# A third-order feature interaction kernel: first chunk in halves, D groups ahead of c1, q weights of chunks 0 to 3 on VectorE

## The chip, the cores and the metric

One core of one Trainium2 chip. A core has TensorE (matmuls, into PSUM), VectorE, ScalarE, GpSimd, and SyncE, which here only issues DMAs. The metric is the device time of one execution in microseconds; lower is better.

## The reference

Input x is (B=512, M=40, D=16). W0, W1, W2 are (40, 40, 100), (40, 100, 100), (40, 100, 100); b0 to b2 have 100 entries, lin_w 300.

```python
curr = x
for Wk, bk in zip([W0, W1, W2], [b0, b1, b2]):
    z = einsum('bid,bjd->bdij', x, curr)
    curr = einsum('bdij,ijh->bhd', z, Wk) + bk[None, :, None]
    logit.append(curr)
out = sum(concatenate(logit, axis=1), axis=-1) @ lin_w + lin_b     # (512, 1)
```

## The kernel before

Only layer 1's output c1 is computed in full. The sum over d makes layers 2 and 3 a quadratic form: out = sum over d and h of c1 times q, where q is a product of the same pairwise terms z with weights D, and D is built on the chip from W1, W2 and lin_w. A constant feature (the 41st) and an extra output column (the 101st, J=101) carry the biases.

**Chunks.** z is symmetric in i and j, so 41 features give some 880 pairs, held as C=7 chunks of K=126 rows. The columns are N=1024: two d values of 512 examples. There are U=8 such column blocks, so NCH=56 chunks, numbered m = 7u + c. For each chunk VectorE forms z = x_a * x_b (`form`, line 246), ScalarE rounds it to the 32-bit matmul type as z_high (`round_high`, L324), and VectorE makes z_low = z - z_high (`split`, L253). TensorE then does three products (high x high, low x high, high x low) in two halves of 512 columns, six matmuls, once with the c1 weights (`c1_chunk`) and once with the q weights (`q_chunk`), both L434. The q products run LAG=8 chunks behind the c1 products.

**x_b.** In chunks 1 to 6 it is picked out of x_a by a selection matmul (`select_xb`, L476). From chunk 7 on it comes by DMA: `load_xb(1, c)` brings x for chunk 7 + c into xb_z[c], once chunk c has been split (low_done), so chunk 9 uses `load_xb(1, 2)`, chunk 10 `load_xb(1, 3)`.

**D.** `v_piece`, `turn_v` and v_sb reduce W2 and lin_w to v. Five D groups (`d_group`, L518 and L521, two matmuls each) multiply W1 by v into two PSUM buffers in turn; ScalarE copies each out (`copy_d`, L338) before its buffer is used again. SyncE and GpSimd store the groups to DRAM (`store_d`, L159), and once all stores have landed nine gathers by SyncE and three by ScalarE (`gather_d`, L153) bring them back in pairs: piece 0 holds the two sides for chunks 0 and 1, piece 1 for chunks 2 to 6. The q weights are the sum of both sides, then rounded (wq_high), then the remainder (wq_low). VectorE does that for chunks 0 and 1 (`first_weights`, L279 to L284), GpSimd for chunks 2 and 3 and for 4 to 6 (L419 to L424).

**Order.** It is written by hand, each engine works through its own list, and semaphores tie them. VectorE's list in the first loop body is form(m), then for m = 9 `first_weights`, then split(m-1). TensorE's list begins with 20 matmuls on zeros (`warm`, L485), selections, v pieces and c1 chunk 0, then D groups 0 and 1, c1 chunk 1, D groups 2 and 3, selection 6, D group 4, c1 chunks 2 to 7, and then q(0), c1(8), q(1), c1(9) and so on. SyncE's list around the change is the part that matters most:

```python
            store_d(sp, 0, LEFT + 4 * GI, 4 * GI, LOWER - 4 * GI, d_stored)
            sp.wait_ge(low_done, 3)
            load_xb(1, 2)
            sp.wait_ge(equals_cleared, 1)
            sp.wait_ge(d_stored, 16 * DS)
            sp.wait_ge(d_stored_pool, 16)
            for side, t, piece in GATHER:
                if piece == 1 and (side, t) == (0, 0):
                    sp.wait_ge(low_done, 4)
                    load_xb(1, 3)
```

Of the kernel before, what the change touches and what calls it, by code (L numbers as in the profile page):

```python
# [42 lines left out]
PREP_AT = 9  # L43
# [5 lines left out]
WARM = 20  # L49
# [10 lines left out]
def build(nc, xa, xw, w0_pairs, w1x, w2h, small, out):  # L60
# [3 lines left out]
    with ExitStack() as ctx:  # L64
# [54 lines left out]
        xa_loaded = [sem(f"xa_loaded{i}") for i in range(2)]  # L119
        w0_loaded = [sem(f"w0_loaded{i}") for i in range(len(WC_CUTS) - 1)]  # L120
# [44 lines left out]
        @block.sync  # L165
        def _(sp):
            def load_xa(u, par):
                sp.dma_start(x_a[:, par, :], xa[:, bass.ds(u * N, N)]).then_inc(xa_loaded[par], 16)

            def load_xb(u, c):  # L170
                sp.dma_start(xb_z[:, c, :], xw[c:c + 128, bass.ds(u * N, N)]).then_inc(xb_loaded[c], 16)

            def load_w0(i):
                cols = slice(WC_CUTS[i] * 2 * J, WC_CUTS[i + 1] * 2 * J)
                sp.dma_start(pair_sb[:, cols], w0_pairs[:, cols]).then_inc(w0_loaded[i], 16)

# [22 lines left out]
            sp.wait_ge(dgroup_copied, 2)  # L199
# [6 lines left out]
            sp.wait_ge(dgroup_copied, NG)  # L206
# [24 lines left out]
            sp.dma_start(out, out_sb[:, :]).then_inc(out_stored, 16)  # L231
            sp.wait_ge(out_stored, 16)

        @block.vector
        def _(dve):
# [34 lines left out]
            def split_x():  # L270
                dve.wait_ge(xa_high, 1)
                nc.vector.tensor_tensor(x_split[LOW_AT:K], x_a[LOW_AT:K, 0, :], x_split[LOW_AT:K].bitcast(fp32),
                                        ALU.subtract).then_inc(xa_split, 1)

            def first_weights():

                cols = slice(PREP_CUTS[0] * J, PREP_CUTS[1] * J)
                dve.wait_ge(dpair_loaded[0], 16 * sum(g[2] == 0 for g in GATHER))
                nc.vector.tensor_tensor(q_sides[0:K, 0, cols], q_sides[0:K, 0, cols], q_sides[0:K, 1, cols],  # L279
                                        ALU.add).then_inc(wq_sums, 1)  # L280
                dve.wait_ge(wq_sums, 1)
                nc.vector.tensor_copy(wq_high[0:K, cols], q_sides[0:K, 0, cols]).then_inc(wq_highs, 1)
                dve.wait_ge(wq_highs, 1)
                nc.vector.tensor_tensor(wq_low[0:K, cols], q_sides[0:K, 0, cols], wq_high[0:K, cols].bitcast(fp32),  # L284
                                        ALU.subtract).then_inc(wq_ready, 1)

            def products(it, m0):
# [12 lines left out]

# [18 lines left out]
        def _(act):  # L319
# [46 lines left out]
            act.wait_ge(dgroup_copied, NG)  # L366
# [24 lines left out]
        def _(pool):  # L391
# [5 lines left out]
            for i in range(len(WC_CUTS)):  # L397
# [5 lines left out]
                if i > 0:  # L403
                    c0, c1 = WC_CUTS[i - 1], WC_CUTS[i]
                    pool.wait_ge(wc_highs, i)
                    nc.gpsimd.tensor_tensor(chunks(wc_low, c0, c1), w0_sides[0:K, c0:c1, 0, :],  # L406
                                            chunks(wc_high, c0, c1).bitcast(fp32), ALU.subtract).then_inc(wc_ready, 1)
            pool.wait_ge(wc_ready, len(WC_CUTS) - 1)
            nc.gpsimd.memset(q_sides[0:P, 1, 0:J], 0.0).then_inc(equals_cleared, 1)
            pool.wait_ge(equals_cleared, 1)  # L410
            pool.wait_ge(dgroup_copied, 4)
            store_d(pool, 1, 0, UPPER - LEFT, LEFT, d_stored_pool, (0, 32))
            for i in range(1, len(PREP_CUTS) - 1):
                cols = slice(PREP_CUTS[i] * J, PREP_CUTS[i + 1] * J)
                if PREP_CUTS[i] in WQ_CUTS:
                    piece = WQ_CUTS.index(PREP_CUTS[i])
                    pool.wait_ge(dpair_loaded[piece], 16 * sum(g[2] == piece for g in GATHER))
                    pool.wait_ge(wq_ready, 1)
                nc.gpsimd.tensor_tensor(q_sides[0:K, 0, cols], q_sides[0:K, 0, cols], q_sides[0:K, 1, cols],  # L419
                                        ALU.add).then_inc(wq_sums, 1)  # L420
                pool.wait_ge(wq_sums, i + 1)
                nc.gpsimd.tensor_copy(wq_high[0:K, cols], q_sides[0:K, 0, cols]).then_inc(wq_highs, 1)
                pool.wait_ge(wq_highs, i + 1)
                nc.gpsimd.tensor_tensor(wq_low[0:K, cols], q_sides[0:K, 0, cols], wq_high[0:K, cols].bitcast(fp32),  # L424
                                        ALU.subtract).then_inc(wq_ready, 1)

        @block.tensor
        def _(pe):
# [77 lines left out]
            def d_group(g):  # L506
# [7 lines left out]
                if g >= 2:  # L514
                    pe.wait_ge(dgroup_copied, g - 1)
# [121 lines left out]
```

## Time and profile before

| | |
|---|---|
| runs of the kernel (3) | median 185.86 us, 185.47 to 185.96 |
| the profiled execution | 186.29 us, its span (first to last instruction) 184.5 us |
| TensorE busy | 175.8 us, 95% of the span |
| VectorE busy | 151.8 us, 82% |
| ScalarE, GpSimd busy | 73.9 us, 16.2 us |
| mean granted TensorE clock | 1.000 |
| DMA | 37.71 MB, mean 204 GB/s |

The span is shorter than the time by 1.79 us, which lie before the first and behind the last instruction. Busy matmuls overlap, so 95% is not the share of its peak. A timeline gives for each instruction, or run of like ones, its start, its duration, and in brackets how long the engine was idle before it and what released it.

### The profile page before, as it was taken

What the parts mean: (1) busy time and instruction counts of PE and PEld (TensorE: products, weight loads), DVE (VectorE), ACT (ScalarE), POOL (GpSimd) and SP (SyncE); (2) the same over time, 40 slices, a digit from 0 to 9 for tenths busy, and PEclk for the clock granted to TensorE, in tenths of its full rate; (3) what the DMA queues carried; (4) which work ended last, traced back from release to release, by engine and by line L of the source; (5) the groups of instructions that cost most, each with busy time, mean ns of one, the idle gap of its engine ahead of it and who ended that gap; (6) DMA issues with size and microseconds to landing.
All of it is one profiled execution on the core that took longest, in us unless ns stands there. A gap on an engine that the chain in (4) does not pass through costs nothing.

```text
span 184.5 us, 2573 instructions
## 1 busy us (share of the span) xinstructions
PE 175.8 (95%) x814; PEld 118.7 (64%) x814; DVE 151.8 (82%) x135; ACT 73.9 (40%) x79; POOL 16.2 (9%) x21
## 2 busy tenths in 40 slices
PE   7798998869999999999999999999999999999994
PEld 2364474546677777777777777777777777777760
DVE  0699698869999999999999999999999999300622
ACT  2554664124444624462446244534453445002001
POOL 3670010087000000000000000000000000000000
PEclk9999999999999999999999999999999999999999
DMA  6999997999797739774986597659765200000000
GB/s 192 379 409 411 412 219 218 231 406 397 230 324 233 234 122 321 247 227 124 331 230 228 126 322 235 223 135 329 228 219 128 99 0 0 0 0 4 0 0 0
DMA packets 11845, 37.71 MB, mean 204 GB/s; under 512 B 2305, under 2 KB 2941, under 8 KB 11838
## 3 DMA queue, kind: packets, MB, share of 16 engines
q1 hardware_dynamic: 11538, 37.38, 62.1%
q0 software_dynamic: 48, 0.16, 0.3%
q10 hardware_dynamic: 252, 0.09, 0.3%
q8 instruction: 4, 0.07, 0.2%
q14 instruction: 3, 0.02, 0.0%
HBM read 36.28 MB, written 1.33 MB: 204 GB/s over the span
## 4 chain that ended last, share of the span: by engine, by line
PE 79%; DMA 8%; SPq 3%; POOL 3%; issue 2%; DVE 1%; ACT 1%; DVEq 0%; ACTq 0%
PE q_ps L434 39%; PE c_ps L434 36%; DMA pair_sb<-d_dram 3%; DMA pair_sb<-w_pairs 3%; DMA d_dram<-w_d 2%; PE q_ps L518 2%; SPq L153 2%; POOL pair_sb L401 1%; POOL wq_low L424 1%; PE q_ps L443 1%; POOL wc_low L406 1%; DVE xb_z L246 1%; ACT z_high L324 1%; SPq L159 1%; PE c_ps L565 1%
## 5 line engine op out<-in xcount | busy, mean ns | idle before, releaser
L324 ACT ACTIVATE z_high<-xb_z 126x1024 fp32r<-126x1024 f32 x56 | 59.2, 1060 | 73.0 <-DVE xb_z L246 69.3
L253 DVE TENSOR_TENSOR z_low<-xb_z,z_high 126x1024 fp32r<-126x1024 f32 x56 | 68.9, 1232 | 1.1 <-ACT z_high L324 0.8
L246 DVE TENSOR_TENSOR xb_z<-x_a,xb_z 126x1024 f32<-126x1024 f32 x50 | 62.1, 1242 | 8.3 <-DMA xb_z<-xw 8.3
L434 PE MATMUL q_ps<-z_high,wq_high 126*101 126x512 f32 x108 | 34.1, 396 | 3.0 <-POOL wq_low L424 1.5
L434 PE MATMUL c_ps<-z_high,wc_high 126*101 126x512 f32 x112 | 35.5, 398 | 0.2 <-issue 0.2
L434 PE MATMUL c_ps<-z_high,wc_low 126*101 126x512 f32 x112 | 35.0, 394 | 0.0
L434 PE MATMUL c_ps<-z_low,wc_high 126*101 126x512 f32 x112 | 35.0, 394 | 0.0
L434 PE MATMUL q_ps<-z_high,wq_low 126*101 126x512 f32 x108 | 33.8, 394 | 0.0
L434 PE MATMUL q_ps<-z_low,wq_high 126*101 126x512 f32 x108 | 33.7, 393 | 0.0
L434 PEld LDWEIGHTS q_ps<-z_high,wq_high 126*101 126x101 f32 x108 | 17.7, 165 | 10.8 <-POOL wq_low L424 2.0
L434 PEld LDWEIGHTS c_ps<-z_high,wc_high 126*101 126x101 f32 x112 | 18.0, 165 | 9.0 <-issue 1.6
L434 PEld LDWEIGHTS c_ps<-z_high,wc_low 126*101 126x101 f32 x112 | 18.5, 165 | 7.5
L434 PEld LDWEIGHTS c_ps<-z_low,wc_high 126*101 126x101 f32 x112 | 18.5, 165 | 7.4
L434 PEld LDWEIGHTS q_ps<-z_high,wq_low 126*101 126x101 f32 x108 | 17.9, 166 | 7.3
L434 PEld LDWEIGHTS q_ps<-z_low,wq_high 126*101 126x101 f32 x108 | 17.8, 165 | 7.2
L261 DVE TENSOR_TENSOR w_post<-q_ps,w_post 101x1024 f32<-101x1024 f32 x7 | 8.5, 1216 | 12.0 <-PE q_ps L434 12.0
L331 ACT ACTIVATE w_post<-c_ps 101x1024 f32<-101x1024 f32 x8 | 8.1, 1010 | 14.1 <-PE c_ps L434 14.1
L263 DVE TENSOR_TENSOR acc<-acc,w_post 101x1024 f32<-101x1024 f32 x7 | 8.6, 1226 | 0.2
L485 PE MATMUL q_ps<-warm_sb 128*128 128x512 bf16 x20 | 6.2, 483 | 1.4 <-POOL warm_sb L393 1.4
L267 DVE TENSOR_TENSOR w_post<-q_ps,w_post 101x256 f32<-101x256 f32 (+1 forms) x3 | 1.4, 508 | 5.2 <-PE q_ps L443 5.2
L388 ACT ACTIVATE out_sb<-c_ps,const_sb 1x512 f32<-1x512 f32 x1 | 0.7, 678 | 12.2 <-PE c_ps L568 12.2
L485 PEld LDWEIGHTS q_ps<-warm_sb 128*128 128x128 bf16 x20 | 2.3, 121 | 4.7 <-issue 2.2
(56 smaller groups left out, 66.1 us busy)
## 6 DMA issues: line engine op xcount, KB each, us to landing
xb_z<-xw SPq DMA_DIRECT2D x50, 512.0 KB, 4.5
x_a<-xa SPq DMA_DIRECT2D x8, 512.0 KB, 5.0
w_d<-w2h SPq DMA_DIRECT2D x4, 512.0 KB, 7.4
w_post<-w1x SPq DMA_DIRECT2D x3, 512.0 KB, 10.0
d_dram<-w_d SPq DMA_DIRECT2D x4, 252.5 KB, 4.3
w_post<-w1x SPq DMA_DIRECT2D x1, 562.5 KB, 12.7
pair_sb<-d_dram SPq DMA_DIRECT2D x6, 82.9 KB
pair_sb<-w_pairs SPq DMA_DIRECT2D x1, 404.0 KB, 5.4
```

The source lines that it names most:

```text
L153: eng.dma_start(q_sides[P * t:P * (t + 1), side, c0 * J:c1 * J].rearrange("p (c j) -> p c j", j=J), src).then_inc(dpair_loaded[piece], 16)
L159: eng.dma_start(d_dram[r0:r1, column * J:(column + n) * J], w2_d[DR * upper + r0:DR * upper + r1, first * J:(first + n) * J]).then_inc(sto ...
L246: nc.vector.tensor_tensor(xb_z[0:K, c, :], x_a[0:K, u % 2, :], x_b, ALU.mult).then_inc(z_done, 1)
L253: nc.vector.tensor_tensor(z_low[0:K, m % SLOTS, :], xb_z[0:K, c, :], z_high[0:K, m % SLOTS, :].bitcast(fp32), ALU.subtract).then_inc(low_d ...
L261: nc.vector.tensor_tensor(prod, q_ps[u % 2][0:J, :], c1_sb[u % 2], ALU.mult).then_inc(q_psum_free, 1)
L263: nc.vector.tensor_tensor(acc[:, :], acc[:, :], prod, ALU.add).then_inc(acc_done, 1)
L324: nc.scalar.activation(z_high[0:K, m % SLOTS, :], xb_z[0:K, m % C, :], ACT.Copy).then_inc(high_done, 1)
L331: nc.scalar.activation(c1_sb[u % 2], c1_ps[u % 2][0:J, :], ACT.Copy).then_inc(c1_copied, 1)
L401: nc.gpsimd.tensor_tensor(side[:, :, 0, :], side[:, :, 0, :], side[:, :, 1, :], ALU.add).then_inc(wc_sums, 1)
L434: last = nc.tensor.matmul(ps[0:J, h * B:(h + 1) * B], w[0:K, c * J:(c + 1) * J], z[0:K, slot, h * B:(h + 1) * B], start=(c == 0 and k == 0 ...
L485: nc.tensor.matmul(warm_ps, warm_sb[:, 0:128], warm_sb[:, :], start=True, stop=True)
L518: last = nc.tensor.matmul(d_ps[g % 2][0:DR, 0:n], v_sb[:, :], w1_post[0:J, first:first + n], start=True, stop=True)
```

## The change

Chunk 0 is loaded, formed, rounded, split and multiplied in two halves of 512 columns, and its c1 weights are prepared on VectorE (they were on GpSimd and ScalarE); 15 warm matmuls run in place of 20. All five D groups come ahead of c1 chunk 1, and groups 1 and 3 are copied out by VectorE, the others by ScalarE. VectorE prepares the q weights of chunks 0 and 1 behind split(9), and those of chunks 2 and 3 behind split(11); GpSimd keeps chunks 4 to 6. On SyncE, the load for chunk 9 moves between the gathers of pieces 0 and 1, and that for chunk 10 behind all gathers.

The diff without semaphore declarations and with some waits left out:

```diff
-PREP_AT = 9
+PREP_AT = (10, 12)
...
-WARM = 20
+WARM = 15
...
-            load_xa(0, 0)
-            load_xb(0, 0)
+            sp.dma_start(x_a[:, 0, 0:B], xa[:, 0:B]).then_inc(xa_first, 16)
+            sp.dma_start(xb_z[:, 0, 0:B], xw[0:128, 0:B]).then_inc(xb_first, 16)
             load_w0(0)
+            sp.dma_start(x_a[:, 0, B:N], xa[:, B:N]).then_inc(xa_loaded[0], 16)
+            sp.dma_start(xb_z[:, 0, B:N], xw[0:128, B:N]).then_inc(xb_loaded[0], 16)
...
-            sp.wait_ge(dgroup_copied, 4)
+            sp.wait_ge(dgroup_copied, 2)
+            sp.wait_ge(dgroup_copied_dve, 2)
             store_d(sp, 0, LEFT + 2 * GI, 2 * GI, 2 * GI, d_stored)
...
-            sp.wait_ge(low_done, 3)
-            load_xb(1, 2)
             sp.wait_ge(equals_cleared, 1)
...
                 if piece == 1 and (side, t) == (0, 0):
-                    sp.wait_ge(low_done, 4)
-                    load_xb(1, 3)
+                    sp.wait_ge(low_done, 3)
+                    load_xb(1, 2)
                 if side == 0 or piece > 0:
                     gather_d(sp, side, t, piece)
-            for c in range(4, C):
+            for c in range(3, C):
                 sp.wait_ge(low_done, c + 1)
...
+            def copy_d(g):
+                dve.wait_ge(dgroup_done, g + 1)
+                nc.vector.tensor_copy(w2_d[:, g * GI * J:(g + 1) * GI * J], d_ps[g % 2]).then_inc(dgroup_copied_dve, 1)
-            def first_weights():
-                cols = slice(PREP_CUTS[0] * J, PREP_CUTS[1] * J)
-                dve.wait_ge(dpair_loaded[0], 16 * sum(g[2] == 0 for g in GATHER))
+            def first_weights(i):
+                cols = slice(PREP_CUTS[i] * J, PREP_CUTS[i + 1] * J)
+                dve.wait_ge(dpair_loaded[i], 16 * sum(g[2] == i for g in GATHER))
...
+            def first_chunk():
+                def form_half(h):
+                    cols = slice(h * B, (h + 1) * B)
+                    return nc.vector.tensor_tensor(xb_z[0:K, 0, cols], x_a[0:K, 0, cols], xb_z[0:K, 0, cols], ALU.mult)
...
+                dve.wait_ge(xa_first, 16)
+                dve.wait_ge(xb_first, 16)
+                form_half(0).then_inc(z_first, 1)
+                dve.wait_ge(w0_loaded[0], 16)
+                nc.vector.tensor_tensor(w0_sides[0:K, 0, 0, :], w0_sides[0:K, 0, 0, :], w0_sides[0:K, 0, 1, :],
+                                        ALU.add).then_inc(first_sums, 1)
...
+                nc.vector.tensor_copy(wc_high[0:K, 0:J], w0_sides[0:K, 0, 0, :]).then_inc(first_highs, 1)
...
+                nc.vector.tensor_tensor(wc_low[0:K, 0:J], w0_sides[0:K, 0, 0, :], wc_high[0:K, 0:J].bitcast(fp32),
+                                        ALU.subtract).then_inc(first_ready, 1)
...
+                split_half(0).then_inc(low_first, 1)
...
+                form_half(1).then_inc(z_done, 1)
+                split_x()
+                dve.wait_ge(high_done, 1)
+                split_half(1).then_inc(low_done, 1)
...
                 for m in range(m0, m0 + BODY):
+                    if m == 5:
+                        copy_d(1)
+                    if m == 0:
+                        first_chunk()
+                        continue
                     form(it, m)
-                    if m == 0:
-                        split_x()
-                        split(it, 0)
+                    if m == 5:
+                        copy_d(3)
...
-                    if m == PREP_AT:
-                        first_weights()
                     if m > 1:
                         split(it, m - 1)
+                    if m in PREP_AT:
+                        first_weights(PREP_AT.index(m))
...
             copy_d(0)
-            copy_d(1)
             round_high(0, 4)
             copy_d(2)
-            copy_d(3)
             copy_d(4)
...
-            for i in range(len(WC_CUTS)):
+            for i in range(1, len(WC_CUTS)):
...
-            for i in range(1, len(PREP_CUTS) - 1):
-                cols = slice(PREP_CUTS[i] * J, PREP_CUTS[i + 1] * J)
...
+            cols = slice(PREP_CUTS[2] * J, PREP_CUTS[3] * J)
+            pool.wait_ge(dpair_loaded[1], 16 * sum(g[2] == 1 for g in GATHER))
...
+            def first_half(h):
+                pe.wait_ge(first_ready, 1)
+                pe.wait_ge(high_first if h == 0 else high_done, 1)
+                pe.wait_ge(low_first if h == 0 else low_done, 1)
+                for k, (w, z) in enumerate(((wc_high, z_high), (wc_low, z_high), (wc_high, z_low))):
+                    nc.tensor.matmul(c1_ps[0][0:J, h * B:(h + 1) * B], w[0:K, 0:J], z[0:K, 0, h * B:(h + 1) * B],
+                                     start=(k == 0), stop=False)
...
+            first_half(0)
             select_xb(1)
             select_xb(2)
+            first_half(1)
             v_piece(0)
-            c1_chunk(0, 0)
             select_xb(3)
...
             d_group(1)
-            c1_chunk(0, 1)
+            select_xb(6)
             d_group(2)
             d_group(3)
-            select_xb(6)
             d_group(4)
-            for m in range(2, LAG):
+            for m in range(1, LAG):
                 c1_chunk(0, m)
```

## Rows read from the trace of the kernel before

**Rows 1.** The page, sections 2 and 4: GB/s per slice; the chain, shares by engine.
```profile
GB/s 192 379 409 411 412 219 218 231 406 397 230 324 233 234 122 321 247 227 124 331 230 228 126 322 235 223 135 329 228 219 128 99 0 0 0 0 4 0 0 0
...
PE 79%; DMA 8%; SPq 3%; POOL 3%; issue 2%; DVE 1%; ACT 1%; DVEq 0%; ACTq 0%
```

**Rows 2.** Timeline, TensorE, 0 to 58 us: start, duration, engine, line, operation, idle before.
```profile
30.97 0.63 PE L434 MATMUL c_ps<-z_low,wc_high 126*101 126x512 f32 x2
...
33.10 0.70 PE L434 MATMUL q_ps<-z_high,wq_high 126*101 126x512 f32 x2 [1.50 <-DVE wq_low L284]
...
38.31 0.63 PE L434 MATMUL c_ps<-z_low,wc_high 126*101 126x512 f32 x2
...
40.44 0.71 PE L434 MATMUL q_ps<-z_high,wq_high 126*101 126x512 f32 x2 [1.50 <-POOL wq_low L424]
```

**Rows 3.** Chain that ended last, in order of time: start, duration, engine and line.
```profile
44.83 1.56 PE c_ps L434 x6
...
46.39 1.39 PE q_ps L434 x6
...
47.78 1.52 PE c_ps L434 x6
```

**Rows 4.** Timeline, VectorE, 0 to 58 us.
```profile
22.49 1.22 DVE L246 TENSOR_TENSOR xb_z<-x_a,q_ps 126x1024 f32<-126x1024 f32 x1 [1.30 <-PE q_ps L476]
...
28.66 1.22 DVE L253 TENSOR_TENSOR z_low<-xb_z,z_high 126x1024 fp32r<-126x1024 f32 x1
...
29.80 1.22 DVE L246 TENSOR_TENSOR xb_z<-x_a,xb_z 126x1024 f32<-126x1024 f32 x1
...
31.88 0.37 DVE L279 TENSOR_TENSOR pair_sb<-pair_sb 126x202 f32<-126x202 f32 x1 [0.87 <-DMA pair_sb<-d_dram]
...
32.59 0.37 DVE L284 TENSOR_TENSOR wq_low<-pair_sb,wq_high 126x202 fp32r<-126x202 f32 x1
...
34.78 1.23 DVE L246 TENSOR_TENSOR xb_z<-x_a,xb_z 126x1024 f32<-126x1024 f32 x1 [0.69 <-DMA xb_z<-xw]
...
41.39 1.87 DVE L246 TENSOR_TENSOR xb_z<-x_a,xb_z 126x1024 f32<-126x1024 f32 x1
```

**Rows 5.** Timeline, SyncE, 22 to 40 us: the DMAs it issues.
```profile
22.38 1.77 SPq L159 DMA_DIRECT2D d_dram<-w_d  x3
...
24.20 0.58 SPq L171 DMA_DIRECT2D xb_z<-xw  x1
...
28.11 1.19 SPq L153 DMA_DIRECT2D pair_sb<-d_dram  x3
...
29.34 0.37 SPq L171 DMA_DIRECT2D xb_z<-xw  x1
...
32.47 1.35 SPq L171 DMA_DIRECT2D xb_z<-xw  x3
```

**Rows 6.** DMA issues at 7.25, 23.5, 29.34, 32.47 us, all x loads: us to landing.
```profile
w_post<-w1x SPq DMA_DIRECT2D x1, 562.5 KB, 12.7
...
d_dram<-w_d SPq DMA_DIRECT2D x1, 25.2 KB, 4.5
...
xb_z<-xw SPq DMA_DIRECT2D x1, 512.0 KB, 5.3
...
xb_z<-xw SPq DMA_DIRECT2D x1, 512.0 KB, 6.1
...
xb_z<-xw SPq DMA_DIRECT2D x50, 512.0 KB, 4.5
```

**Rows 7.** Timeline, TensorE, 0 to 58 us: D group 3.
```profile
20.70 0.59 PE L518 MATMUL q_ps<-w_post,v_sb 101*64 101x505 f32 x1
```

**Rows 8.** Timeline, GpSimd, 0 to 58 us.
```profile
37.61 0.61 POOL L419 TENSOR_TENSOR pair_sb<-pair_sb 126x202 f32<-126x202 f32 x1 [14.00 <-DMA pair_sb<-d_dram]
```

**Rows 9.** Two windows of the warm matmuls: first column TensorE busy us (matmuls).
```profile
1.36:4.75 3.39, 3.39 (x8) 1.20 (x9) 0.00 (x0) 0.68 (x2) 0.84 (x1) 1.00 0.86 276
4.75:7.56 2.81, 2.81 (x13) 1.13 (x11) 1.45 (x2) 1.27 (x2) 1.21 (x1) 1.00 1.02 365
```

More of the change, by code:

```diff
@@ L119, in build @@
         xa_loaded = [sem(f"xa_loaded{i}") for i in range(2)]
+        xa_first, xb_first = sem("xa_first"), sem("xb_first")
+        z_first, high_first, low_first = sem("z_first"), sem("high_first"), sem("low_first")
+        first_sums, first_highs, first_ready = sem("first_sums"), sem("first_highs"), sem("first_ready")
         w0_loaded = [sem(f"w0_loaded{i}") for i in range(len(WC_CUTS) - 1)]
@@ L131, in build @@
         dgroup_done, dgroup_copied = sem("dgroup_done"), sem("dgroup_copied")
+        dgroup_copied_dve = sem("dgroup_copied_dve")
         wc_sums, wc_highs, wc_ready = sem("wc_sums"), sem("wc_highs"), sem("wc_ready")
         wq_sums, wq_highs, wq_ready = sem("wq_sums"), sem("wq_highs"), sem("wq_ready")
+        last_sums, last_highs, last_ready = sem("last_sums"), sem("last_highs"), sem("last_ready")
         filled, equals_cleared = sem("filled"), sem("equals_cleared")
@@ L198, in _ @@
                 load_xb(1, c)
-            sp.wait_ge(dgroup_copied, 2)
+            sp.wait_ge(dgroup_copied, 1)
+            sp.wait_ge(dgroup_copied_dve, 1)
             store_d(sp, 0, LEFT, 0, 2 * GI, d_stored)
@@ L279, in first_weights @@
+            def first_weights(i):
+                cols = slice(PREP_CUTS[i] * J, PREP_CUTS[i + 1] * J)
+                dve.wait_ge(dpair_loaded[i], 16 * sum(g[2] == i for g in GATHER))
                 nc.vector.tensor_tensor(q_sides[0:K, 0, cols], q_sides[0:K, 0, cols], q_sides[0:K, 1, cols],
                                         ALU.add).then_inc(wq_sums, 1)
-                dve.wait_ge(wq_sums, 1)
+                dve.wait_ge(wq_sums, i + 1)
                 nc.vector.tensor_copy(wq_high[0:K, cols], q_sides[0:K, 0, cols]).then_inc(wq_highs, 1)
-                dve.wait_ge(wq_highs, 1)
+                dve.wait_ge(wq_highs, i + 1)
@@ L284, in first_weights, with split_half @@
                 nc.vector.tensor_tensor(wq_low[0:K, cols], q_sides[0:K, 0, cols], wq_high[0:K, cols].bitcast(fp32),
                                         ALU.subtract).then_inc(wq_ready, 1)
+            def first_chunk():
+                def form_half(h):
+                    cols = slice(h * B, (h + 1) * B)
+                    return nc.vector.tensor_tensor(xb_z[0:K, 0, cols], x_a[0:K, 0, cols], xb_z[0:K, 0, cols], ALU.mult)
+                def split_half(h):
+                    cols = slice(h * B, (h + 1) * B)
+                    return nc.vector.tensor_tensor(z_low[0:K, 0, cols], xb_z[0:K, 0, cols],
+                                                   z_high[0:K, 0, cols].bitcast(fp32), ALU.subtract)
+                dve.wait_ge(xa_first, 16)
[4 more added lines that the diff above has]
+                                        ALU.add).then_inc(first_sums, 1)
+                dve.wait_ge(first_sums, 1)
+                nc.vector.tensor_copy(wc_high[0:K, 0:J], w0_sides[0:K, 0, 0, :]).then_inc(first_highs, 1)
+                dve.wait_ge(first_highs, 1)
+                nc.vector.tensor_tensor(wc_low[0:K, 0:J], w0_sides[0:K, 0, 0, :], wc_high[0:K, 0:J].bitcast(fp32),
+                                        ALU.subtract).then_inc(first_ready, 1)
+                dve.wait_ge(high_first, 1)
+                dve.wait_ge(z_slots_free, 1)
+                split_half(0).then_inc(low_first, 1)
+                dve.wait_ge(xa_loaded[0], 16)
+                dve.wait_ge(xb_loaded[0], 16)
+                form_half(1).then_inc(z_done, 1)
+                split_x()
+                dve.wait_ge(high_done, 1)
+                split_half(1).then_inc(low_done, 1)
@@ L339, in copy_d @@
                                      ACT.Copy).then_inc(dgroup_copied, 1)
-            act.wait_ge(xa_loaded[0], 16)
-            nc.scalar.activation(x_split[0:K], x_a[0:K, 0, :], ACT.Copy).then_inc(xa_high, 1)
-            round_high(0, 0)
+            for h in range(2):
+                cols = slice(h * B, (h + 1) * B)
+                act.wait_ge(xa_first if h == 0 else xa_loaded[0], 16)
+                nc.scalar.activation(x_split[0:K, cols], x_a[0:K, 0, cols], ACT.Copy).then_inc(xa_high, 1)
+                act.wait_ge(z_first if h == 0 else z_done, 1)
+                act.wait_ge(z_slots_free, 1)
+                nc.scalar.activation(z_high[0:K, 0, cols], xb_z[0:K, 0, cols], ACT.Copy
+                                     ).then_inc(high_first if h == 0 else high_done, 1)
             act.wait_ge(small_loaded, 16)
             nc.scalar.activation(select_r[:, :], select_sb, ACT.Copy).then_inc(select_rounded, 1)
-            for i in range(len(WC_CUTS) - 1):
-                act.wait_ge(wc_sums, i + 1)
+            for i in range(1, len(WC_CUTS) - 1):
+                act.wait_ge(wc_sums, i)
                 nc.scalar.activation(chunks(wc_high, WC_CUTS[i], WC_CUTS[i + 1]),
@@ L360, in _ @@
             copy_d(0)
-            copy_d(1)
             round_high(0, 4)
             copy_d(2)
-            copy_d(3)
             copy_d(4)
-            act.wait_ge(dgroup_copied, NG)
+            act.wait_ge(dgroup_copied, 3)
+            act.wait_ge(dgroup_copied_dve, 2)
             for m in range(5, BODY):
@@ L402, in _ @@
                                             ALU.add).then_inc(wc_sums, 1)
-                if i > 0:
+                if i > 1:
                     c0, c1 = WC_CUTS[i - 1], WC_CUTS[i]
-                    pool.wait_ge(wc_highs, i)
+                    pool.wait_ge(wc_highs, i - 1)
                     nc.gpsimd.tensor_tensor(chunks(wc_low, c0, c1), w0_sides[0:K, c0:c1, 0, :],
                                             chunks(wc_high, c0, c1).bitcast(fp32), ALU.subtract).then_inc(wc_ready, 1)
-            pool.wait_ge(wc_ready, len(WC_CUTS) - 1)
+            pool.wait_ge(first_ready, 1)
@@ L409, in _ @@
+            pool.wait_ge(wc_ready, len(WC_CUTS) - 2)
             nc.gpsimd.memset(q_sides[0:P, 1, 0:J], 0.0).then_inc(equals_cleared, 1)
             pool.wait_ge(equals_cleared, 1)
-            pool.wait_ge(dgroup_copied, 4)
+            pool.wait_ge(dgroup_copied, 2)
+            pool.wait_ge(dgroup_copied_dve, 2)
             store_d(pool, 1, 0, UPPER - LEFT, LEFT, d_stored_pool, (0, 32))
-            for i in range(1, len(PREP_CUTS) - 1):
-                cols = slice(PREP_CUTS[i] * J, PREP_CUTS[i + 1] * J)
[L415 to L425, printed above, removed]
@@ new lines, in _ @@
+            cols = slice(PREP_CUTS[2] * J, PREP_CUTS[3] * J)
+            pool.wait_ge(dpair_loaded[1], 16 * sum(g[2] == 1 for g in GATHER))
+            nc.gpsimd.tensor_tensor(q_sides[0:K, 0, cols], q_sides[0:K, 0, cols], q_sides[0:K, 1, cols],
+                                    ALU.add).then_inc(last_sums, 1)
+            pool.wait_ge(last_sums, 1)
+            nc.gpsimd.tensor_copy(wq_high[0:K, cols], q_sides[0:K, 0, cols]).then_inc(last_highs, 1)
+            pool.wait_ge(last_highs, 1)
@@ L427, in _ @@
+            nc.gpsimd.tensor_tensor(wq_low[0:K, cols], q_sides[0:K, 0, cols], wq_high[0:K, cols].bitcast(fp32),
+                                    ALU.subtract).then_inc(last_ready, 1)
         @block.tensor
@@ L448, in c1_chunk @@
                 u, c = divmod(m, C)
-                if m in WC_CUTS[:-1]:
-                    pe.wait_ge(wc_ready, WC_CUTS.index(m) + 1)
+                if m in WC_CUTS[1:-1]:
+                    pe.wait_ge(wc_ready, WC_CUTS.index(m))
                 pe.wait_ge(high_done, it * BODY + (m + 1))
@@ L457, in c1_chunk @@
                     last.then_inc(c1_done, 1)
+            def first_half(h):
[5 more added lines that the diff above has]
+                                     start=(k == 0), stop=False)
             def q_chunk(it, m):
                 u, c = divmod(m, C)
-                if m in PREP_CUTS[:-1]:
+                if m in PREP_CUTS[:2]:
                     pe.wait_ge(wq_ready, PREP_CUTS.index(m) + 1)
+                if m == PREP_CUTS[2]:
+                    pe.wait_ge(last_ready, 1)
                 if c == 0:
@@ L513, in d_group @@
                     pe.wait_ge(w1_loaded[W1_CUTS.index(g)], 16)
-                if g >= 2:
-                    pe.wait_ge(dgroup_copied, g - 1)
+                if g in (2, 4):
+                    pe.wait_ge(dgroup_copied, g // 2)
+                if g == 3:
+                    pe.wait_ge(dgroup_copied_dve, 1)
                 n = (GI if g < NG - 1 else 1) * J
```

4 lines of the change are left out of this document (2 added, 2 removed).

## The prediction

> **What bounds the kernel now.** I read the chain that ended last first: 79% of it is TensorE and 8% DMA [rows 1]. TensorE's timeline then shows where that engine was not fed: once the D groups are done it stops twice, ahead of the first q product (the pair issued at 30.97 is followed by one at 33.10) and ahead of the third (38.31, then 40.44); between and behind them pairs follow each other every 0.46 to 0.47 us [rows 2]. Both stops name a wait for split q weights, the first made by VectorE, the second by GpSimd. In the chain of waits every chunk from 40.44 to the tail costs 1.39 us, apart from two of 1.56 and 1.52, where VectorE had delivered the low part just in time [rows 3]. So the end is set by one number: when the first q product starts. It starts at 33.10 and the span ends at 184.50, 151.40 us later. Of these, 40.44 - (38.31 + 0.46) = 1.67 us are the second stop and 1.56 + 1.52 - 2 x 1.39 = 0.30 us the late low parts. An undisturbed run from the first q product to the end is 151.40 - 1.67 - 0.30 = 149.4 us.
>
> VectorE's timeline shows who makes the first q weights and what it waits for: chunk 7's split at 28.66, chunk 9's product at 29.80, the weights from 31.88 to 32.96 (32.59 + 0.37), chunk 10's product at 34.78, behind a DMA of x [rows 4]. SyncE's timeline gives those DMAs: chunk 9's x is issued at 24.20, while the D stores fly; three gathers follow from 28.11, chunk 10's x at 29.34, six gathers from 29.76, then the x of chunks 11 to 13 from 32.47 [rows 5].
>
> **The start (half chunks, weights of chunk 0 on VectorE, fewer warm matmuls).** It puts chunk 0's first three matmuls (0.7 us) ahead of the first selection and takes GpSimd's chunk-0 operations off ScalarE's way. Halved operations cost VectorE a little more than half of a whole one's 1.14 us of spacing, and the three operations on chunk 0's 101 columns less than the 1.08 us that such three take on 202 [rows 4]; I cost them at -0.6 to +0.5 us for the moment v is ready, and take -0.6, because six chunk-0 matmuls behind v_piece(0) shrink to three. None of it reaches the end directly: the D groups hang on more than v, since group 3 needs the last piece of w1, issued at 7.25 and landing 12.7 us later, at 19.95 [rows 6], and the same bytes stand ahead of it as before. SyncE's two more DMA issues (0.42 us each) and 256 KB transfers in place of 512 KB lie beside that queue: 0 to +0.3 us, taken as 0.
>
> **D groups ahead of c1, copies shared.** Group 3's matmuls start at 20.70 now [rows 7] and its store is issued at 22.38 [rows 5]. Taking c1 chunk 1 (1.4 us) out from between lets them start just behind the weights' landing, 19.95 + 0.05: 0.7 us sooner, and the copy on VectorE costs about what ScalarE's does (0.65 against 0.6). VectorE now stands in its queue for that copy from about 19.9 to 21.0, with split(4) and chunk 6 behind it; now it waits there 1.3 us for the selection of chunk 6 (the product at 22.49 [rows 4]), so little is lost. Stores, their landing (4.5 us behind the last issue [rows 6]) and the gathers all move by -0.7: the gathers start at 28.11 - 0.7 = 27.4. Bounds of this shift: 0 (w1 later by what the added issues cost, stores as slow) and -1.3 (the stores see a queue that is emptier by one x load).
>
> **The x loads.** Here the sum turns. Before, chunk 9's x goes out ahead of the gathers, chunk 10's between the two pieces. After, chunk 9's takes the middle place and chunk 10's comes behind all nine gathers of SyncE. By the same spacings as [rows 5]: chunk 9's x is issued at 27.4 + (29.34 - 28.11) = 28.6 and, with the 5.3 us of the load that has this place now [rows 6], lands at 33.9, not 29.7. Chunk 10's is issued at 27.4 + (32.47 - 28.11) = 31.8 and, with the 6.1 us of the load in that place [rows 6], lands at 37.9. One load of 512 KB less is in flight when the gathers begin, which may bring up to 1.3 us (its bytes at the 409 to 412 GB/s of the fullest slices [rows 1]); but the slices in which the gathers begin are among the emptiest of that stretch (219 to 231 GB/s), so the queue is not what holds them, and I take 0.3: 37.6.
>
> **The order on VectorE.** Before, the first weights stand behind chunk 9's product, so they need chunk 9's x. After, they stand behind chunk 10's product and chunk 9's split. VectorE finishes split(7) at about 29.7, as now (28.66 + 1.14 = 29.80), waits to 33.9 for chunk 9's x, forms it, splits chunk 8, and waits again to 37.6. Then: form(10) and split(9), 1.15 each, the three weight operations 31.88 to 32.96 = 1.08, and 0.14 to TensorE's first matmul at 33.10 [rows 2, 4]: 37.6 + 3.5 = 41.1. GpSimd prepares chunks 4 to 6 in the same microseconds (its gather lands at 37.61 now [rows 8]), and the VectorE operation at 41.39, which ran beside it, took 1.87 us instead of 1.22 [rows 4]; one or two such meetings add 0 to 0.8, I take 0.4. The first q product starts at 41.5 instead of 33.10. Behind it the weights of chunks 2 and 3 cost form, split, form, split and 1.08 us, ready at 41.4 + 4 x 1.14 + 1.08 = 47.0, when TensorE has two q and two c1 chunks of 1.39 us to do until 47.1 at the earliest; the second stop is gone and VectorE, which ran on through the stall, is ahead at chunks 11 and 12. GpSimd's chunks 4 to 6 are ready by then.
>
> **The sum.** 41.5 + 149.4 = 190.9 us of span. TensorE stands still from about 31.1 (c1 chunk 7) to 41.5, over 10 us, where no stop inside the trace exceeds 1.7. The two stops in [rows 2] left the spacing at 0.46 per pair. The nearest row to a long one is the start: out of rest, 8 matmuls of 512 columns took 3.39 us (0.42 each, the 1.2 GHz level), then 13 took 2.81 (0.216 each, 2.4 GHz) [rows 9], although the granted clock reads 1.00 over both. That start cost 3.39 / 2 = 1.7 us. The price after a 10 us rest is thus between 0 and 1.7; I take 1.7, as such a rest is nearer to the start than to a 1.5 us gap. 192.6 us of span, plus 186.29 - 184.50 = 1.79 around it, is 194.4 against the profiled 186.29. The median of the runs is 0.43 below the profiled run, so I predict **194.0**.
>
> The Trainium skill, "TensorE: Matmul & The Clock Gate", Part 1, says that an idle array is put back to the 1.2 GHz level and that only sustained work releases it. By that rule the result is 194.0, without it 192.3; the short gaps of this trace cannot tell, and its start agrees with the rule.
>
> **Rivals.**
> (a) *The clock holds* through the stall: 192.3. For it: the granted clock reads 1.00 everywhere. Against: so it does over the slow start [rows 9].
> (b) *Chunk 10's x is not held up behind the gathers.* With the 4.5 us that such a load takes in the median [rows 6] it lands at 31.8 + 4.5 = 36.3, 1.3 us sooner than taken: 192.7. Against: the load in this very place took 6.1.
> (c) *The D groups come no sooner* (the change doesn't bring what its second part says): group 3 still waits for w1, the stores for their latency, and the gathers start at 28.1: 194.7. With full contention on VectorE and no relief in the queue it reaches 195.5 to 196.
> (d) *Faster: the q wait vanishes.* If the gathers were so early that chunk 10's x landed before VectorE needed it, the first q product would follow c1 chunk 7 at 31.1: 31.1 + 149.4 + 1.36 = 181.9. It decides if the first q product starts before 33.10 + 1.97 = 35.1, so if chunk 10's x lands by 31.6. It is issued at 31.8. Only gathers that start over 5 us sooner would save it, and they hang on w1's landing at 19.95.
>
> **How the numbers follow.** Forecast 194.0: 0.57. (a) 0.12, (b) 0.11, (c) with the heavier contention 0.16, (d) 0.04. (a) and (b) together would be 191.0, (c) at its worst 196; I set the range at 191.0 to 196.6. About 0.3% is what a measurement of this kernel can tell from no change; only (d) lies on the other side: faster 0.04, same 0.01, slower 0.95.
>
> **What would show it.** In the timeline after: TensorE idle for about 10 us between c1 chunk 7 and the first q product, released by VectorE's wq_low; VectorE idle twice ahead of its xb_z products, 4 us and some 1.5 us, both on DMA xb_z<-xw; SyncE issuing one x load between its third and fourth gather and the next behind the ninth; no second stop; about four pairs of matmuls near 0.85 us instead of 0.46 right behind the stall (if the clock falls). I am wrong if the first q product starts below 36, or if VectorE does not wait for x ahead of its first weights.

## The result and the profile after

The changed kernel takes 195.31 us (median of 4 runs, 195.14 to 195.72) against 185.73 before: a ratio of 1.052, 95% interval 1.0495 to 1.0544. The forecast was 194.0, with 191.0 to 196.6 as its range. The profiled execution took 195.14 us, its span 193.4. Ratios and intervals, here and below, are of fast executions alone and can differ from the quotient of the two medians (in experiment 1: 1.025 against 1.030).

TensorE's timeline after, for [rows 2]:

```profile
31.82 0.62 PE L483 MATMUL c_ps<-z_low,wc_high 126*101 126x512 f32 x2
42.50 1.17 PE L483 MATMUL q_ps<-z_high,wq_high 126*101 126x512 f32 x2 [10.06 <-DVE wq_low L295]
43.47 1.05 PE L483 MATMUL q_ps<-z_high,wq_low 126*101 126x512 f32 x2
44.33 1.05 PE L483 MATMUL q_ps<-z_low,wq_high 126*101 126x512 f32 x2
45.18 0.98 PE L483 MATMUL c_ps<-z_high,wc_high 126*101 126x512 f32 x2
45.99 0.62 PE L483 MATMUL c_ps<-z_high,wc_low 126*101 126x512 f32 x2
```

One stop of 10.06 us stands where two of 1.5 stood, and it waits for VectorE's wq_low. The first q product starts at 42.50, 9.40 later than before. From there to the end are 193.4 - 42.5 = 150.9 us: the 149.4 of the prediction and 1.5 more, which lie in the four pairs behind the stop (0.97, 0.86, 0.85, 0.81 from start to start instead of 0.46). 9.40 - 1.97 + 1.5 = 8.9 us is the whole difference of the spans.

VectorE's timeline after, for [rows 4]:

```profile
29.53 1.22 DVE L260 TENSOR_TENSOR z_low<-xb_z,z_high 126x1024 fp32r<-126x1024 f32 x1
33.83 1.23 DVE L253 TENSOR_TENSOR xb_z<-x_a,xb_z 126x1024 f32<-126x1024 f32 x1 [3.09 <-DMA xb_z<-xw]
34.98 1.22 DVE L260 TENSOR_TENSOR z_low<-xb_z,z_high 126x1024 fp32r<-126x1024 f32 x1
38.29 1.33 DVE L253 TENSOR_TENSOR xb_z<-x_a,xb_z 126x1024 f32<-126x1024 f32 x1 [2.10 <-DMA xb_z<-xw]
39.54 1.84 DVE L260 TENSOR_TENSOR z_low<-xb_z,z_high 126x1024 fp32r<-126x1024 f32 x1
41.30 0.36 DVE L290 TENSOR_TENSOR pair_sb<-pair_sb 126x202 f32<-126x202 f32 x1
41.69 0.27 DVE L293 CAST wq_high<-pair_sb 126x202 fp32r<-126x202 f32 x1
41.99 0.37 DVE L295 TENSOR_TENSOR wq_low<-pair_sb,wq_high 126x202 fp32r<-126x202 f32 x1
```

The two waits for x are there, 3.09 and 2.10 us (some 4 and 1.5 were forecast), ahead of the products of chunks 9 and 10; the weights stand behind both. The first is shorter because VectorE itself was later: split(7) starts at 29.53 instead of 28.66, behind the copy of D group 3, which VectorE could start only at 22.12. SyncE's timeline and the two DMA answers that carry the times, for [rows 5, 6] (last piece of w1; then chunk 9's x), and D group 3 on TensorE, for [rows 7]:

```profile
22.88 1.81 SPq L164 DMA_DIRECT2D d_dram<-w_d  x3
28.26 1.19 SPq L158 DMA_DIRECT2D pair_sb<-d_dram  x3
29.49 0.37 SPq L176 DMA_DIRECT2D xb_z<-xw  x1
29.91 2.61 SPq L158 DMA_DIRECT2D pair_sb<-d_dram  x6
32.56 1.81 SPq L176 DMA_DIRECT2D xb_z<-xw  x4
```

```profile
w_post<-w1x SPq DMA_DIRECT2D x1, 562.5 KB, 12.5
...
xb_z<-xw SPq DMA_DIRECT2D x1, 512.0 KB, 4.2
```

```profile
21.01 0.64 PE L580 MATMUL q_ps<-w_post,v_sb 101*64 101x505 f32 x1 [0.52 <-DMA w_post<-w1x]
```

Chunk 9's x is issued at 29.49 instead of 24.20, chunk 10's at 32.56 instead of 29.34. The gathers start at 28.26, no sooner than before (28.11), since w1's last piece, issued at 8.47 (before: 7.25), landed some 12.5 us later, at 20.97, and D group 3 ran at 21.01. The clock, for [rows 9], by windows (the first figure behind the start and end is the length of the window, then come TensorE's busy time and matmuls; the third figure from the end is the granted clock):

```profile
33.00:38.00 5.00, 0.00 (x0) 0.00 (x0) 2.36 (x2) 1.06 (x1) 0.77 (x1) 0.77 1.08 238
38.00:43.00 5.00, 0.50 (x1) 0.41 (x2) 4.64 (x6) 1.06 (x1) 2.15 (x3) 0.50 1.03 411
42.50:47.00 4.50, 4.50 (x13) 3.16 (x14) 4.50 (x5) 2.25 (x3) 0.00 (x0) 0.62 1.01 387
```

It falls during the stop, to 0.50, the 1.2 GHz level, and comes back behind it (0.78 on average from 45.5 to 46.5, 1.00 from 46.5 to 48.0).

### The profile page after: what moved, and what is told of

Same layout as the page of the kernel before. It is cut to its first block, busy times and chain, and to the rows that moved or that the text cites. A ratio compares the mean times of both kernels' runs of the same rounds, so it can differ in the third digit from the quotient of the medians.

```text
span 193.4 us, 2575 instructions
## 1 busy us (share of the span) xinstructions
PE 176.2 (91%) x809; PEld 119.4 (62%) x809; DVE 153.7 (80%) x145; ACT 73.5 (38%) x78; POOL 9.5 (5%) x16
## 4 chain that ended last, share of the span: by engine, by line
PE 77%; DMA 12%; SPq 6%; DVE 3%; issue 2%; ACT 0%; DVEq 0%
PE q_ps L483 40%; PE c_ps L483 35%; DMA w_post<-w1x 6%; DMA xb_z<-xw 3%; DMA d_dram<-w_d 2%; SPq L158 2%; SPq L184 1%; DVE z_low L260 1%; SPq L188 1%; PE q_ps L492 1%; SPq L180 1%; PE q_ps L580 1%; SPq L164 1%; PE c_ps L627 1%; PE c_ps L630 0%
## 5 line engine op out<-in xcount | busy, mean ns | idle before, releaser
L371 ACT ACTIVATE z_high<-xb_z 126x1024 fp32r<-126x1024 f32 x55 | 58.4, 1062 | 76.7 <-DVE xb_z L253 70.1
L260 DVE TENSOR_TENSOR z_low<-xb_z,z_high 126x1024 fp32r<-126x1024 f32 x55 | 67.6, 1230 | 0.7 <-ACT z_high L371 0.7
L253 DVE TENSOR_TENSOR xb_z<-x_a,xb_z 126x1024 f32<-126x1024 f32 x49 | 59.8, 1221 | 5.2 <-DMA xb_z<-xw 5.2
L483 PE MATMUL c_ps<-z_high,wc_high 126*101 126x512 f32 x110 | 35.0, 399 | 0.1
L483 PE MATMUL c_ps<-z_low,wc_high 126*101 126x512 f32 x110 | 34.4, 394 | 0.0
L483 PE MATMUL c_ps<-z_high,wc_low 126*101 126x512 f32 x110 | 34.4, 393 | 0.0
L545 PE MATMUL q_ps<-warm_sb 128*128 128x512 bf16 x15 | 5.2, 521 | 1.4 <-POOL warm_sb L444 1.4
L580 PE MATMUL q_ps<-w_post,v_sb 101*64 101x505 f32 (+1 forms) x10 | 4.2, 535 | 0.9 <-DMA w_post<-w1x 0.5
## 6 DMA issues: line engine op xcount, KB each, us to landing
w_post<-w1x SPq DMA_DIRECT2D x1, 562.5 KB, 12.5
```

Of the source, the lines that this page charges most:

```text
L253: nc.vector.tensor_tensor(xb_z[0:K, c, :], x_a[0:K, u % 2, :], x_b, ALU.mult).then_inc(z_done, 1)
L260: nc.vector.tensor_tensor(z_low[0:K, m % SLOTS, :], xb_z[0:K, c, :], z_high[0:K, m % SLOTS, :].bitcast(fp32), ALU.subtract).then_inc(low_d ...
L371: nc.scalar.activation(z_high[0:K, m % SLOTS, :], xb_z[0:K, m % C, :], ACT.Copy).then_inc(high_done, 1)
L483: last = nc.tensor.matmul(ps[0:J, h * B:(h + 1) * B], w[0:K, c * J:(c + 1) * J], z[0:K, slot, h * B:(h + 1) * B], start=(c == 0 and k == 0 ...
L545: nc.tensor.matmul(warm_ps, warm_sb[:, 0:128], warm_sb[:, :], start=True, stop=True)
L580: last = nc.tensor.matmul(d_ps[g % 2][0:DR, 0:n], v_sb[:, :], w1_post[0:J, first:first + n], start=True, stop=True)
```

## The experiments

Ratios are to the kernel before on the same chip, with 95% intervals; its median was 185.67 to 185.92 there. "Put back" means undone in the changed kernel.

**1. The x loads put back.**

```diff
+            sp.wait_ge(low_done, 3)
+            load_xb(1, 2)
             sp.wait_ge(equals_cleared, 1)
...
-                    load_xb(1, 2)
+                    load_xb(1, 3)
```

> The changed kernel with SyncE's x loads back in their old places (chunk 9's ahead of the gathers, chunk 10's between the two pieces). My theory: the loss is the stall ahead of the first q product, made by the late x loads and by the weights' place behind split(9). Chunk 10's x then lands near 34, and form, split and the weights (3.4 us) put the first q product at 37.5 instead of 42.5: 5.0 us back, with 1.4 us lost again ahead of the third q product, whose weights still stand behind split(11). 190.0 if the clock holds over a 5 us idle, 191.7 without any relief of the clock. Rival (the start in halves or the D copies on VectorE cost the time): within 1 us of 195.3.

191.32 us, ratio 1.025 (1.017 to 1.034).

**2. The first weights put back.**

```diff
                     form(it, m)
+                    if m == 9:
+                        first_weights(0)
                     if m > 1:
                         split(it, m - 1)
-                    if m in PREP_AT:
-                        first_weights(PREP_AT.index(m))
+                    if m == 12:
+                        first_weights(1)
```

> The changed kernel with only the weights of chunks 0 and 1 back in their old place, ahead of split(8). My theory: they then need chunk 9's x alone (33.8), so the first q product starts at 36.2, 6.3 us sooner; but the weights of chunks 2 and 3 still stand behind split(11) and are ready near 46.8, so the third q product, at 49.7 in the changed kernel, comes only 2.8 us sooner: 192.5. Rival (the x loads alone make the stall): no gain, 195.3.

194.05 us, ratio 1.039 (1.029 to 1.049).

TensorE's timeline in experiment 1, then in experiment 2:

```profile
32.12 0.62 PE L485 MATMUL c_ps<-z_low,wc_high 126*101 126x512 f32 x2
37.87 1.17 PE L485 MATMUL q_ps<-z_high,wq_high 126*101 126x512 f32 x2 [5.13 <-DVE wq_low L297]
38.84 1.05 PE L485 MATMUL q_ps<-z_high,wq_low 126*101 126x512 f32 x2
```

```profile
36.99 0.70 PE L485 MATMUL q_ps<-z_high,wq_high 126*101 126x512 f32 x2 [3.80 <-DVE wq_low L295]
...
38.27 1.06 PE L485 MATMUL q_ps<-z_low,wq_high 126*101 126x512 f32 x2
...
47.61 0.96 PE L485 MATMUL q_ps<-z_high,wq_high 126*101 126x512 f32 x2 [3.26 <-DVE wq_low L295]
48.36 1.05 PE L485 MATMUL q_ps<-z_high,wq_low 126*101 126x512 f32 x2
```

Experiment 1 went about as expected: the first q product came 4.6 us sooner (5.0 expected), with the clock falling over a stop of 5.13 us too. Here it stayed low for seven pairs, to 43.96, some 2.8 us more than at the usual 0.46 us per pair. The wait ahead of the third q product did not come, because the slow matmuls used that time: its weights were ready at 45.28, and it started at 46.34. Experiment 2 missed by 1.5 us, with runs that scatter from 192.07 to 194.95. Its first q product is at 36.99 (36.2 expected), its third at 47.61, 2.1 us sooner than in the changed kernel (2.8 expected). The clock fell twice, around stops of only 3.80 and 3.26 us (pairs 0.85 apart from 38.27 and from 48.36 on), which I had not counted; the second fall takes back some 1.6 us.

**3. Both put back**, the weights of chunks 2 and 3 behind split(9) (`m == 10` in the last `if` of experiment 2).

> Both of these, with VectorE's weights of chunks 2 and 3 behind split(9), so that everything of the change is kept but the x loads and the weights' places. My theory: first q product at 33.3, third at 38.9, chunk 10's low part some 1 us late: 185.4, equal to the kernel before within 0.6 us. Rival (start and D groups ahead of c1 are worth the time they seem to save, about 1 to 2 us): 184.0. Rival (they cost): 187 or more.

186.55 us, ratio 1.0046 (1.0013 to 1.0079): all of the loss but 0.9 us is back (the kernel before took 185.67 beside it). That is 1.1 us above the 185.4 expected and just under the 187 of the second rival. First q product at 33.39; in place of the stop ahead of the third, one of 1.37 us ahead of c1 chunk 10, whose split stood behind the weights:

```profile
33.39 0.70 PE L487 MATMUL q_ps<-z_high,wq_high 126*101 126x512 f32 x2 [0.56 <-DVE wq_low L297]
...
42.19 0.69 PE L487 MATMUL c_ps<-z_high,wc_high 126*101 126x512 f32 x2 [1.37 <-DVE z_low L262]
```
With everything else of the change in it, this kernel is not faster than the one before.

**4. TensorE kept busy in the stop.**

```diff
             for m in range(1, LAG):
                 c1_chunk(0, m)
+            pe.wait_ge(dgroup_copied, 3)
+            for _ in range(45):
+                warm()
```

> The changed kernel with 45 matmuls on zeros (9.7 us) behind c1 chunk 7, inside the stall of 10.1 us. Theory: the clock's fall to 1.2 GHz in the stall costs 1.6 us, in the first seven or eight matmuls behind it; with the engine kept busy these run at 0.23 us each: 193.7. Rival (the slow matmuls behind the stall have another cause, late data or weights): 195.3.

193.76 us (193.47 to 194.04), ratio 1.040 (1.033 to 1.048), mean clock 1.0. TensorE's timeline:

```profile
32.84 9.66 PE L545 MATMUL q_ps<-warm_sb 128*128 128x512 bf16 x44
42.67 0.71 PE L483 MATMUL q_ps<-z_high,wq_high 126*101 126x512 f32 x2 [0.17 <-DVE wq_low L295]
```

**5. The x loads' order alone, in the kernel before** (the reverse of experiment 1's edit).

> The kernel before with the x loads alone in their new places. My theory: chunk 9's x lands at 34.6 and holds the first weights, which stand behind chunk 9's product: first q product at 37.0 instead of 33.1, third near 43.3 instead of 40.4, and the clock falls in the 5.4 us idle (1.6 us): 189.8. Rival (it takes the weights' new place as well to lose anything): within 1 us of 185.7.

188.68 us, ratio 1.0185 (1.015 to 1.022). Slower as the theory has it; 1.1 less than expected, since chunk 9's x landed at 33.4, and the first q product started at 35.77 and not at 37.0. VectorE's row, then TensorE's:

```profile
33.42 1.23 DVE L244 TENSOR_TENSOR xb_z<-x_a,xb_z 126x1024 f32<-126x1024 f32 x1 [3.29 <-DMA xb_z<-xw]
```

```profile
35.77 1.17 PE L432 MATMUL q_ps<-z_high,wq_high 126*101 126x512 f32 x2 [3.94 <-DVE wq_low L282]
```

**6. D groups and q weights alone, in the kernel before**; start, x loads and the first weights' place are the old ones, the copies of the D groups those of the change.

```diff
                     if m == PREP_AT:
-                        first_weights()
-                    if m > 1:
+                        first_weights(0)
+                    if m > 1 and m != 11:
                         split(it, m - 1)
+                    if m == 10:
+                        split(it, 10)
+                        first_weights(1)
...
             d_group(1)
-            c1_chunk(0, 1)
+            select_xb(6)
             d_group(2)
             d_group(3)
-            select_xb(6)
             d_group(4)
```

> The kernel before with two parts of the change alone: D groups ahead of c1 (copies shared with VectorE), and the q weights of chunks 2 and 3 on VectorE, behind split(9) and split(10); start, x loads and the place of the first weights as before. My theory: the halved start sends w1 out 1 us later (its last piece landed at 20.95 in the changed kernel, 19.95 before), and that is why the D groups gained nothing. With the old start D group 3 runs at 20.0, the gathers start at 27.4, the first q product at 32.5 and the third near 38.2: 183.4. Rival (D's stores and gathers set the pace whatever w1 does): no sooner than the run that has the q weights alone on VectorE, 184.2.

**7. The same with the halved start kept.**

> As the run with both put back, the halved start kept, and split(10) moved ahead of the weights of chunks 2 and 3. Theory: takes the 1.4 us wait of c1 chunk 10 away and puts 0.2 us ahead of the third q product: 185.3. If the halved start is what costs, this stays 1.5 to 2 us above the run with the old start; if the start is worth its own 0.7 us of matmuls, it is below it.

**8. The q weights of chunks 2 and 3 alone on VectorE, in the kernel before.**

> The kernel before with the q weights of chunks 2 and 3 on VectorE alone, behind split(9) and split(10). Theory: they are ready at about 38.9 instead of 40.4, and VectorE's slow operations beside GpSimd shrink: 1.3 to 1.6 us off, 184.2. Rival (chunk 11's product, pushed back, makes c1 chunk 11 late by as much): 185.7.

| | us | ratio |
|---|---|---|
| 6: D groups and q weights | 184.75 | 0.9936 (0.9913 to 0.9959) |
| 7: with the halved start | 186.27 | 1.0033 (1.0006 to 1.0061) |
| 8: q weights alone | 185.22 | 0.9979 (0.9954 to 1.0003) |

All three ran on one chip. Each came out 1.0 to 1.4 us above its expectation (183.4, 185.3 and 184.2). Experiment 8 is not told apart from the kernel before: its weights for the third q product were ready at 40.68 and not at 38.9. Between 8 and 6 only the D groups differ (their place and their copies): the gathers start 0.71 us sooner (27.40 against 28.11), and the medians differ by 0.5 us, with intervals that just touch. Between 6 and 7 only the start differs (half loads, halved work, c1 weights on VectorE, 15 warm matmuls): it costs 1.5 us. TensorE's timeline at D group 3 and the first and third q product, in experiment 6, then in 7:

```profile
20.14 0.64 PE L533 MATMUL q_ps<-w_post,v_sb 101*64 101x505 f32 x1 [0.30 <-DMA w_post<-w1x]
...
33.03 0.70 PE L445 MATMUL q_ps<-z_high,wq_high 126*101 126x512 f32 x2 [1.43 <-DVE wq_low L292]
...
39.87 0.71 PE L445 MATMUL q_ps<-z_high,wq_high 126*101 126x512 f32 x2 [1.01 <-DVE wq_low L292]
```

```profile
21.31 0.64 PE L585 MATMUL q_ps<-w_post,v_sb 101*64 101x505 f32 x1 [0.30 <-DMA w_post<-w1x]
...
34.45 0.70 PE L488 MATMUL q_ps<-z_high,wq_high 126*101 126x512 f32 x2 [1.70 <-DVE wq_low L297]
...
41.29 0.70 PE L488 MATMUL q_ps<-z_high,wq_high 126*101 126x512 f32 x2 [1.00 <-DVE wq_low L297]
```

D group 3 waits for w1 in both, and gets it 1.17 us later with the halved start; both q products come 1.42 us later. The windows from 3 to 9 us, of 6 and then of 7, end with the DMA engines' busy share and GB/s:

```profile
3.00:9.00 6.00, 4.80 (x19) 2.11 (x18) 3.06 (x3) 2.65 (x5) 2.55 (x3) 1.00 1.03 392
```

```profile
3.00:9.00 6.00, 4.41 (x15) 1.66 (x13) 3.85 (x7) 2.72 (x5) 0.22 (x1) 1.00 0.96 325
```

The engines are a little less busy, and move 325 GB/s instead of 392: 0.4 MB less in 6 us, which is 1 us at 410 GB/s. The busy share alone (0.96 against 1.03; it can read a little over 1) would account for an estimated 27 of these 67 GB/s. SyncE is later too: it issues the last piece of w1 at about 8.9 instead of 7.08, and it lands 12.3 instead of 13.0 us later. So the two added issues, which the prediction put beside the queue, do stand ahead of w1. Experiment 6 is faster than the kernel before by 0.6%, less than expected: its gathers start at 27.40 as worked out, but piece 0 lands at 31.8, and VectorE, held up beside GpSimd, had the third q product's weights ready only at 39.8.

**9 and 10. Experiment 6 with the weights ahead of split(10)**; in 9 GpSimd's weights also wait for them.

```diff
                     if m == 10:
-                        split(it, 10)
                         first_weights(1)
+                        split(it, 10)
...
             pool.wait_ge(dpair_loaded[1], 16 * sum(g[2] == 1 for g in GATHER))
+            pool.wait_ge(wq_ready, 2)
```

> The run with the old start, with the weights of chunks 2 and 3 ahead of split(10) instead of behind it, and GpSimd's weights of chunks 4 to 6 only after them. Theory: there the gather landed at 35.9 and VectorE was in two splits beside GpSimd until 38.0, so the third q product came at 39.9; now the weights are ready at 37.4, the third q product follows the first four chunks at 38.6, and chunk 11 costs 0.3 us: 183.8. Rival (VectorE is short of time here, whatever its order): 184.8.

> The same without GpSimd's wait. If GpSimd's work beside VectorE's costs time there, the three weight operations take 1.8 instead of 1.1 us and split(10) some 0.4 more: 0 to 0.4 us above the run with the wait, 184.0.

185.40 us, ratio 0.997 (0.994 to 0.999), and 185.01, ratio 0.996 (0.994 to 0.998). The expectations were 183.8 and 184.0, and the run without the wait was to be the slower one; it is not. The three weight operations take 1.1 us with the wait and 1.8 without, as expected, but with it GpSimd's operations only move beside VectorE's next ones (xb_z 3.24 us for two, split 1.85). The stop ahead of the third q product is gone and comes back as one of 1.13 us (with the wait) or 0.23 and 0.54 us (without) ahead of c1 chunks, for VectorE's splits. Their intervals and that of experiment 6 overlap, so no order of these is shown to win. That fits the rival of 9, that VectorE is short of time here whatever its order.

**11. Chunk 0 loaded whole, worked on in halves** (`load_xa(0, 0)`, `load_xb(0, 0)` in experiment 7).

> The run with the halved start kept and split(10) ahead, with chunk 0's x_a and x_b loaded whole (two DMAs of 512 KB, as before) and still worked on in halves. My theory: the four DMAs of 256 KB move fewer bytes per us (325 GB/s against 392 between 3 and 9 us with the engines as busy), which is what delays w1 by 1 us; loaded whole, w1's last piece lands at 20.0 instead of 20.9, D group 3 runs at about 20.6 (v is ready later, since the halves of chunk 0 start at 6.1), 0.3 to 0.8 us off 186.3: 185.7. Rival (v's chain, not w1, is what is late with the halved start): w1 lands sooner but the time rises, to 187.

187.88 us, ratio 1.0056 (1.0016 to 1.0097).

```profile
3.00:9.00 6.00, 5.62 (x15) 1.89 (x13) 3.17 (x7) 2.00 (x4) 1.22 (x2) 1.00 1.03 398
```

```profile
10.73 1.18 PE L539 MATMUL c_ps<-z_high,select_r 126*128 126x512 f32 x2 [1.87 <-DVE z_high L279]
...
19.10 0.64 PE L583 MATMUL q_ps<-w_post,v_sb 101*64 101x505 f32 x1 [0.37 <-ACT v_sb L411]
```

The DMA moves 398 GB/s from 3 to 9 us, and w1's last piece lands at about 18.7, against about 21.2 in experiment 7: four transfers of 256 KB in place of two of 512 KB are what delays w1 (whether by their shorter rows or by the two more issues was not separated). But v is 2.2 us later (D group 0 at 19.10 instead of 16.87), and the time does not fall to the 185.7 expected. Whether it rises, as the rival said, is not shown: the interval overlaps that of experiment 7, on another chip, and in six of the seven runs the clock fell for a moment (mean 0.989 to 0.991; in the profiled one at the start); the one run without that took 185.43.

## Why the prediction was right

The mechanism was right, and the size within 1.3 us; one term of the sum was wrong, and two agreements are in part luck.

**The x loads** were the step that decided. They land at 33.8 and 38.2, against 33.9 and 37.6 worked out. The first agreement is luck: that load was issued 0.9 us later than worked out and took 4.2 us instead of 5.3. The second is the one that sets the first q product; experiments 1 and 5 show their order alone to be worth 4.0 us in the changed kernel and 2.9 us in the one before. **The order on VectorE**: 38.29 to 42.50 is 4.2 us, against 3.5 + 0.4; one split beside GpSimd took 1.84 us. Put back alone, the x order brings 4.0 us (experiment 1) and the weights' place 1.3 (experiment 2), both together 8.8 (experiment 3). That they are more together than in sum has three causes, whose shares were not separated: the weights wait for whichever x stands ahead of them, each of the first two still pays for the clock, and experiment 3 also moved the later weights forward. **The run behind the first q product**, 149.4 us, came out at 149.3 in experiment 4. **The clock**: 1.7 us taken, 1.6 measured. By the rule of "TensorE: Matmul & The Clock Gate" in the Trainium skill, Part 1, its fall in the stop was to be expected. Here the trace agrees: 0.50 granted in the stop. Rival (a) is out. That the price came so close is in part luck: it was taken from another stretch, and in experiment 1 the same fall cost some 2.8 us.

**What was off** is one term, the shift of the D groups. I took -0.7 us; the gathers came 0.15 us later than before. The step "the same bytes stand ahead of it" costed the four half loads at 0 to +0.3 us; w1 came 1.0 us later, and by experiments 6 and 7 the start costs 1.2 us at D group 3, as fewer bytes per us are moved early on and w1 is issued later. With the old start the D groups do bring their 0.7 us (experiment 6). The moment v is ready was off as well, 0.5 us later than before (D group 0 at 16.90 instead of 16.43) where 0.6 sooner was taken; it did not decide, since D group 3 waited for w1. So the D groups did what rival (c) says, which had a chance of 0.16, and the measured 195.31 lies nearer its 194.7 to 196 than the forecast. (Its heavier case is overstated: 194.7 + 0.4 for the contention + 0.3 for the queue are 195.4, not 195.5 to 196.) With +0.85 for the gathers and +0.3 for VectorE, less 0.1 for the load, the first q product moves from 41.5 to 42.5, and the time from 194.0 to 195.0.

Rival (b) did not show: 5.6 us to landing, near the 6.1 of that place. Rival (d) failed where it had to: chunk 10's x was issued at 32.56.

## What to carry to other kernels

Follow a moved DMA issue through to the in-order engine that waits for it: a load that goes behind others in the issuing queue delays everything listed behind its consumer, related or not, so put urgent work ahead of an instruction that waits for a load (experiments 1 and 5). Ask of every long stop what it does to TensorE's clock as well. A part that starts its own work sooner, like halved first loads, can delay the bulk transfer that sets a later stage (experiments 6 and 7).

## What the hardware showed that was not expected

- The clock fell for stops as short as 3.8 and 3.3 us (experiment 2), while the stops of 1.5 us in the kernel before and one of 2.40 in experiment 8 left it alone. In experiment 2 it fell only once TensorE was at work again: it reads 1.00 from 33.0 to 37.5, past the end of the first stop, and 0.50 from 38.3 to 41.0. In experiment 11 it fell behind a stop of 1.87 us: 0.52 from 10.7 to 12.6, ahead of which TensorE had been busy for 1.62 us in 3.73; the first selection pair took 1.18 us.
- From 3 to 9 us the DMA engines moved 298 to 325 GB/s in the six kernels with the loads of 512 columns (busy share 0.90 to 0.96), and 374 to 398 in the seven with those of 1024 (1.01 to 1.03).
- VectorE and GpSimd slow each other down. Beside GpSimd's weight operations VectorE's operations on 1024 columns took up to 1.87 us instead of 1.22 (the kernel before), its cast of 202 columns 0.78 instead of 0.27 (experiments 3 and 10); GpSimd's subtraction of 303 columns took 1.69 us instead of 0.83 (experiment 9 against 6).
